# Storing the low part of one w1 tile 64 bytes lower, in both feed-forwards of a two-layer network

## The reference

```python
# layer 0
h = film(rmsnorm(x, norm1_w), cond, film1_w, film1_b)
x = x + attention(h)                      # one head of 256
h = film(rmsnorm(x, norm2_w), cond, film2_w, film2_b)
x = x + gelu(h @ mlp_w1 + mlp_b1) @ mlp_w2 + mlp_b2     # 256 -> 1024 -> 256
# layer 1
x = x + gate_msa * attention16(modulate(ln(x)))         # 16 heads of 16
x = x + gate_mlp * (gelu(modulate(ln(x)) @ w_mlp1 + b_mlp1) @ w_mlp2 + b_mlp2)
```

## The kernel before

|---|---|---|
| w1 hi | 221056 (128) | 106368 (128) |
| w1 lo | 212864 (128) | 114560 (128) |
| w2 hi | 202304 (64) | 140864 (64) |
| w2 lo | 194112 (64) | 149056 (64) |
| m_h_hi, m_h_lo (two each) | 97856, 99904, 101952, 104000 (all 64) | the same |
| g_hi, g_lo (four each) | all (128) | all (128) |

## Time and profile before

### The profile page before, as it was taken

The page is one execution under the profiler, slowest core; times in us unless marked ns, Lnnn a source line. Parts: engine busy times, 40 slices in busy tenths (PEclk is TensorE's granted clock), DMA queues, the critical chain, the costliest instruction groups (busy, mean ns, idle before and its releaser), DMA issues.

```text
span 1594.8 us, 42633 instructions
## 1 busy us (share of the span) xinstructions
PE 1560.0 (98%) x14314; PEld 1399.4 (88%) x14314; DVE 1307.9 (82%) x2953; ACT 846.7 (53%) x1696; POOL 483.1 (30%) x639
## 2 busy tenths in 40 slices
PE   8999999999999999999999999999997999999999
PEld 7999998999999998677777777777775999999999
DVE  5798888787777777788888888888885888888886
ACT  3566664343333343667777767776666333333333
POOL 2333322131111223243433434433333322222221
PEclk9999999999999999999999999999999999999999
DMA  5600002111111112333333333333331232222222
GB/s 175 216 21 20 20 20 72 66 43 52 40 53 39 53 41 65 107 107 98 108 106 106 112 96 106 105 102 111 100 104 63 80 100 92 94 90 94 89 94 68
DMA packets 147362, 132.72 MB, mean 83 GB/s; under 512 B 23552, under 2 KB 129984, under 8 KB 147280
## 3 DMA queue, kind: packets, MB, share of 16 engines
q1 hardware_dynamic: 147120, 131.61, 25.9%
q0 software_dynamic: 160, 0.04, 0.1%
HBM read 54.61 MB, written 24.54 MB: 50 GB/s over the span
## 4 chain that ended last, share of the span: by engine, by line
PE 89%; DVE 6%; issue 2%; DMA 1%; ACT 1%; SPq 0%; DVEq 0%; ACTq 0%; POOL 0%; POOLq 0%
PE bank L209 61%; PE bank L1733 8%; PE bank L1715 7%; PE bank L1677 5%; PE bank L1743 2%; PE bank L393 2%; DVE D_g_hi L1084 1%; PE bank L1751 1%; PE bank L765 1%; PE bank L465 1%; DVE D_g_lo L1086 1%; PE bank L191 1%; ACT D_g L1076 0%; PE bank L556 0%; DMA A_w_film<-in_L_cond_film_w 0%
## 5 line engine op out<-in xcount | busy, mean ns | idle before, releaser
L1824 ACT ACTIVATE C_probs<-bank 128x1024 f32<-128x1024 f32 x256 | 262.7, 1026 | 157.6 <-PE bank L1715 157.2
L1689 DVE TENSOR_REDUCE C_negmax<-bank 128x4 f32<-128x1024 f32 x248 | 303.4, 1223 | 48.5 <-PE bank L1677 44.6
L1076 ACT ACTIVATE D_g<-bank,D_bias 128x256 f32<-128x256 f32 x256 | 107.5, 472 | 223.0 <-PE bank L209 212.3
L1076 ACT ACTIVATE B_g<-bank,B_bias 128x256 f32<-128x256 f32 x256 | 107.5, 471 | 222.2 <-PE bank L209 222.2
L358 POOL TENSOR_TENSOR m_small<-m_small,consts 128x2 f32<-128x2 f32 x64 | 48.9, 763 | 476.9 <-DVE m_small L349 239.4
L209 PE MATMUL bank<-D_wt_w_hi,D_g_lo 128*128 128x256 f32 x512 | 144.7, 283 | 3.8 <-DVE D_g_lo L1086 3.4
L209 PE MATMUL bank<-B_wt_w_hi,B_g_lo 128*128 128x256 f32 x512 | 144.8, 283 | 3.2 <-DVE B_g_lo L1086 3.0
L1715 PEld LDWEIGHTS bank<-C_qs,C_kx 64*128 64x128 f32 x1024 | 77.3, 185 | 78.7 <-ACT C_probs L1824 46.0
L209 PE MATMUL bank<-m_h_hi,B_wt_w_lo 128*128 128x256 f32 x512 | 143.6, 281 | 0.0
L209 PE MATMUL bank<-B_wt_w_lo,B_g_hi 128*128 128x256 f32 x512 | 143.4, 280 | 0.0
L209 PE MATMUL bank<-B_wt_w_hi,B_g_hi 128*128 128x256 f32 x512 | 143.4, 280 | 0.0
(11 more groups left out here) (263 smaller groups left out, 4931.4 us busy)
## 6 DMA issues: line engine op xcount, KB each, us to landing
C_qs<-C_q_hi SPq DMA_DIRECT2D x128, 128.0 KB
C_kx<-C_k_hi SPq DMA_DIRECT2D x128, 128.0 KB, 2.6
C_qs<-C_q_lo SPq DMA_DIRECT2D x64, 128.0 KB
C_kx<-C_k_lo SPq DMA_DIRECT2D x64, 128.0 KB, 2.1
C_gbc<-mod_rows SPq DMA_DIRECT2D x32, 256.0 KB, 3.4
D_gbc<-mod_rows SPq DMA_DIRECT2D x32, 256.0 KB, 3.4
turned<-N_blocks SPq DMA_DIRECT2D x31, 256.0 KB, 2.0
N_back<-turned SPq DMA_DIRECT2D x124, 64.0 KB, 2.0
```

The lines of the kernel that those rows point to most:

```text
L1076: ins = eng.activation(o, p, func, bias=per_seq(bias1, 2 * u + d, b))
L1689: e_max.by(eng.tensor_reduce(m4[:, :, :, j], spair[:, :].rearrange("p (e q k) -> p e q k", e=2, q=TH), AX, ALU.max, negate=True))
L1824: e_exp.by(eng.activation(probs[t % NP][:, :], stpair[:, :], ACT.Exp, scale=scl))
```

## The change

In both feed-forwards the low part of w1 tile 0 is stored first in the buffer `lo`, and the other 15 tiles behind it with 16 elements (64 bytes) of unused room between. `lo` begins 64 bytes lower than before, so that tile 0 of it lies at remainder 64 and the other tiles lie, in B, exactly where they were. In D the buffers `lo` and `hi` change places: `lo` from 106304 (64; its other tiles from 106880, 128), `hi` from 114560 (128). To keep everything else in its place, the small buffer `consts` (32 bytes) is given up (its values move into unused columns of `a_small` and `m_small`), the gap of 64 bytes `gap2` goes, `gap_m` grows by 32 bytes, and the layer 1 `bcol` moves into the temporary room of phase B. w2, g, m_h and the buffers of C keep their addresses.

`emit_lo` makes two instructions instead of one for the part that holds tile 0 (128 columns, and 384 columns); the other parts stay one instruction each. Reading and order on PE are unchanged.

```diff
+LEAD, LEAD_GAP = (0,), 16
...
-            def __init__(self, sb, sem, name, view):
+            def __init__(self, sb, sem, name, view, lead=(), lo_first=False):
...
+                self.lead, self.rest = list(lead), [i for i in tiles if i not in lead]
+                self.rest_at = len(lead) * P + (LEAD_GAP if lead else 0)
...
+                n = self.t * self.N
+                if self.lo_first:
+                    self.lo = sb("wt_" + self.name + "_lo", [P, n + self.rest_at - len(self.lead) * P], F32R)
+                self.hi = sb("wt_" + self.name + "_hi", [P, n], F32R)
+                if not self.lo_first:
+                    self.lo = sb("wt_" + self.name + "_lo", [P, n + self.rest_at - len(self.lead) * P], F32R)
...
+                for start, group in ((0, self.lead), (self.rest_at, self.rest)):
+                    mine = [i for i in group if part * n <= i * P < (part + 1) * n]
...
+                    ins = eng.tensor_tensor(self.lo[:, o:o + len(mine) * P].rearrange("p (i c) -> p i c", c=P),
+                                            raw[:, src], hi[:, src].bitcast(F32), ALU.subtract)
+                ins.then_inc(self.s_lo, 1)
...
+                    o = self.lead.index(i) * P if i in self.lead else self.rest_at + self.rest.index(i) * P
+                return self.hi[:, c:c + n], self.lo[:, o:o + n]
...
-        scale1m, consts = sb("scale1m", [P, KT * NB]), sb("consts", [P, 8])
-        neghalf, one_rows, zero_col = consts[:, 0:TH], consts[:, TH:TH + 1], consts[:, TH + 1:TH + 2]
+        scale1m = sb("scale1m", [P, KT * NB])
+        neghalf, one_rows, zero_col = small["a_"][:, 22:24], small["m_"][:, 22:23], small["m_"][:, 23:24]
...
-                sb("gap_m", [P, 8])
+                sb("gap_m", [P, 16])
...
-                self.bcol = sb("bcol", [P, HT])
                 if not layer:
+                    self.bcol = sb("bcol", [P, HT])
                     sb("gap1", [P, 16])
-                self.w = [Weight(sb, sem, "w1", a[n1])]
+                self.w = [Weight(sb, sem, "w1", a[n1], LEAD, layer == 1)]
...
-                sb_tmp("next_rest", [P, 448])
+                sb_tmp("next_rest", [P, 448 - HT])
+                mlp.bcol = sb_tmp("next_bcol", [P, HT])
...
-            sb_near("gap2", [P, 16])
```

More of the change, by code:

```diff
@@ L147, in build @@
         class Weight:
-            def __init__(self, sb, sem, name, view):
+            def __init__(self, sb, sem, name, view, lead=(), lo_first=False):
                 self.view, self.t, self.N = view, view.shape[0] // P, view.shape[1]
+                tiles = range(self.t * self.N // P)
+                self.lead, self.rest = list(lead), [i for i in tiles if i not in lead]
+                self.rest_at = len(lead) * P + (LEAD_GAP if lead else 0)
+                self.lo_first = lo_first
                 self.name, self.raw = name, None
@@ L159, in place @@
             def place(self, sb):
-                self.hi = sb("wt_" + self.name + "_hi", [P, self.t * self.N], F32R)
-                self.lo = sb("wt_" + self.name + "_lo", [P, self.t * self.N], F32R)
+                n = self.t * self.N
[4 more added lines that the diff above has]
+                    self.lo = sb("wt_" + self.name + "_lo", [P, n + self.rest_at - len(self.lead) * P], F32R)
             def place_raw(self, sb):
@@ L182, in emit_lo @@
                     eng.wait_ge(self.s_read, readers)
-                eng.tensor_tensor(self.lo[:, c], self.raw[:, c], self.hi[:, c].bitcast(F32), ALU.subtract).then_inc(self.s_lo, 1)
-            def part(self, k, c0, n):
-                return self.hi[:, k * self.N + c0:k * self.N + c0 + n], self.lo[:, k * self.N + c0:k * self.N + c0 + n]
+                if not self.lead:
+                    eng.tensor_tensor(self.lo[:, c], self.raw[:, c], self.hi[:, c].bitcast(F32), ALU.subtract).then_inc(self.s_lo, 1)
+                    return
+                raw, hi = (t[:, :].rearrange("p (i c) -> p i c", c=P) for t in (self.raw, self.hi))
+                for start, group in ((0, self.lead), (self.rest_at, self.rest)):
+                    mine = [i for i in group if part * n <= i * P < (part + 1) * n]
+                    if not mine:
+                        continue
+                    step = mine[1] - mine[0] if len(mine) > 1 else 1
+                    src = slice(mine[0], mine[-1] + 1, step)
+                    o = start + group.index(mine[0]) * P
+                    ins = eng.tensor_tensor(self.lo[:, o:o + len(mine) * P].rearrange("p (i c) -> p i c", c=P),
+                                            raw[:, src], hi[:, src].bitcast(F32), ALU.subtract)
+                ins.then_inc(self.s_lo, 1)
+            def part(self, k, c0, n):
+                c = k * self.N + c0
+                o = c
+                if self.lead:
+                    assert n == P
+                    i = c // P
+                    o = self.lead.index(i) * P if i in self.lead else self.rest_at + self.rest.index(i) * P
+                return self.hi[:, c:c + n], self.lo[:, o:o + n]
         def shift_bias(eng, psum, col, w, c0, shift):
```

## The result

| | before | after |
|---|---|---|
| runs of the first measurement, us | 1600.56, 1588.55, 1587.48, 1587.78 | 1604.09, 1606.84, 1605.34, 1602.65 |
| median, us | 1588.16 | 1604.71 |
| span of the profiled execution, us | 1594.8 | 1602.3 |

The ratio is 1.0082, 95% interval 1.0048 to 1.0116: 0.8% longer, beyond the interval though inside the 1% that the prediction called about the same; 16.5 us between the medians, but only 7.5 us between the spans of the two profiled executions. The time lies outside the predicted range of 1586 to 1600 us.

A forecast was written before the change was run, and what follows sets the result against it. PE's stream of products was taken to bound the kernel. From the profiled 1596.58 us, B's long stretch -4.5, D's first sequences +1.7, D's end +0.6 and B's end +0.4 summed to -1.8: 1594.8 us, range 1586 to 1600.

The forecast's parts named there:

- The first product of a sequence: Both feed-forwards: new difference 0 turns the spacing over between 113 and 118 ns a product; two sequences take 22.21 us.
- the 55 places: Places in the earlier trace, outside the feed-forwards, where difference 0 turned the spacing over: 27 from 118, 28 from 113.
- The period of 256 bytes: Address differences were taken to repeat every 256 bytes, so the new 256 modulo 512 counted as a true 0.
- Cover in B: In B, DVE waits 2.5 us a sequence, so it can follow a PE gain of 0.43 us.
- B's long stretch: B, 338 to 587.5 us: 22 sequences go from 11.31 to 11.11 us each, -4.5 us.
- D's end: D, 1557.4 to 1594.8 us: three undisturbed sequences at 113 ns a product lose +0.6 us.
- B's start: B, 248 to 338 us: waits leave either spacing about half and half; 0, with 1.7 us to either side.
- D's loop: D, 1329 to 1557.4 us: waits for DVE draw the spacing anew; taken as 0, 1.1 us at most either side.
- The reading of the 8 us: Median 8.0 us below the profiled execution: the median runs were taken to have B at 113 ns a product.
- capture rival: Feed-forwards: difference 0 holds the stream at 118 ns a product and 113 is lost; +6.4, 1603.0 us; chance 0.13.
- addresses do nothing: Rival: the stream passes the new difference undisturbed and the time stays that of before, 1588.6 us; chance 0.12.
- the turning over: Main forecast: each difference 0 switches between 113 and 118 ns a product, so sequences alternate; 1594.8 us; chance 0.40.

The follow-up runs named there:

- f_own0: D's w1 tile 0 at 64 as in the change; from sequence 4 down 2's last product streams a w2 copy at remainder 0: 1598.34 us, one run.
- f_prev0: Moved buffers with tile 0 at remainder 128; in D from sequence 4 down 2's last product streams a w2 copy at 128: 1599.38 us beside 1596.92.
- s2: Low parts of w1 tiles 0, 2, 4, 6 at various remainders, without layer 0's second bias: 1589.87 us beside 1596.92, one run each.
- b_look2: The kernel before, unchanged, profiled again: 1593.46 us.
- b_look3: The kernel before, unchanged, profiled again: 1599.84 us.
- again_change: The change itself measured again on another chip, against the kernel before: 1604.12 us, ratio 1.0040.
- e_d_only: The change with tile 0 at remainder 64 in layer 1 only, 128 in layer 0: 1601.80 us, ratio 1.0017 to the kernel before.
- e_control: The change's moved buffers, but tile 0 at remainder 128, keeping address difference 64: 1599.97 us against 1600.04 before, ratio 0.9989.
- e_32: The change with tile 0 at remainder 96 in both layers, difference 32: 1590.76 us, ratio 0.9943 to the kernel before.
- best: Tile 0 at remainder 96 in D; in B in its own buffer at remainder 224, difference 160: 1590.19 us, ratio 0.9949.

## Why the prediction was wrong

- **The step that failed** is the one in "The first product of a sequence", where the own difference was called open and the new difference then taken for a true 0 like the 55 places. Those had the own difference 64, and were 0 modulo 512 against the product before. With both at 0 the stream doesn't turn over but is captured in 118: 100 of 100 and 108 of 108. The 55 places let the stream out of 118 at each of their 27 chances, the change at none of 108. Which of the two unlike properties does it, the own difference or the 256 modulo 512 against the product before, stays open: f_own0 (own 0, 64 before it) doesn't capture, f_prev0 (0 modulo 512 before it, own 64) doesn't either, both with the product of `twin` beside them, and 256 modulo 512 with an own difference of 64 was not run.
- **The period of 256 bytes** held for a stream that comes at 113: the 0 modulo 512 of s2 pushes it to 118 as the 256 of the change does. For a stream that comes at 118 it isn't tested.
- **Cover in B**: read rightly. In b_look2 B runs at 113 with PE busy for all of its 206.70 us, so DVE follows there.
- **B's long stretch**: -4.5 expected, 0 against the profiled execution (214.9 for 214.8 us), +8.2 against an execution at 113 (206.7 in b_look2, 19 sequences).
- **D, sequences 2 to 8**: +3.1 us for seven sequences, 0.44 each; I had +1.7 for eight by alternation. The size of a sequence was right, the alternation not.
- **D's end** (sequence 28 to the last product): 45.1 us before, 46.6 after; +1.5 for +0.6. This stretch is drawn too: b_look3, with difference 64, has 46.6.
- **D's first sequence** was to stay at 118 by its new difference of 192. In after, again_change and e_d_only it went from 118 to 113; the next first product took it back, so that nothing of it reaches the sum.
- **B's start**, taken as 0 with 1.7 to either side: 112.2 us before, 114.3 after. Over the ten profiles with difference 64 in layer 0 it is 111.6 to 113.8, mean 112.6; over the three with 0 114.1 to 114.4, so +1.7. Part of this is the clock and not the address. Five of the ten have a granted clock of 0.98 or 0.99 there and take 113.2 us in the mean, the other five have 1.00 and take 111.9; the three with 0 all have 0.99. At like clock the difference is 1.1 us. The waits still let the stream out at 113, but each first product now takes it back.
- **D's loop**: 0 expected, 217.1 to 217.4 us. Most of what PE loses in `up` 0 comes out of its waits for `D_g_lo`: PE is busy 1.2 us longer (215.97 for 214.80) and waits 1.5 us less. The lines of PE's waits for DVE over D's sequences 9 to 27 (total, times, longest), of after first, then of before:

```profile
PE bank L237 <- DVE D_g_lo L1114: 0.4, 1, 0.4
```

```profile
PE bank L209 <- DVE D_g_lo L1086: 1.9, 7, 0.4
```

- **The splitting of the low part**: the lines view has 6.2 us of POOL for D's w1 low instead of 5.9, and B's on DVE unchanged at 1.4. e_control has the moved buffers and one instruction, e_32 has the moved buffers and the two instructions of the change; neither shows a cost.
- **The reading of the 8 us** (1588 us are executions with B at 113) held: b_look2. I had not seen that D's first stretch is drawn as well; four of the five further profiles of the kernel before have it at 118.
- **The price of the capture rival** was 1603.0 us, measured 1604.7 and 1604.1. I gave it 0.13 because the earlier trace rows showed turns both ways, and had named the own difference as what they lacked. With that unlike row unresolved, the turning over was too sure at 0.40, and the range stopped at 1600 short of the one rival on the other side.
- **The rival "addresses do nothing"** fell: e_32 and the change differ in 32 bytes of one tile, with 1590.8 to 1591.1 us for one and 1604.1 for the other. The rule of two independent read ports in the Trainium skill ("TensorE: Matmul & The Clock Gate", section "Step-by-step: what each phase is for") doesn't cover this: the traces disagree by 4.5 ns a product (117.8 beside 113.3) between these two kernels.

The 16.5 us between the medians of the first measurement then follow from an execution with B and D at 113 as their "before": 8.2 (B, 19 sequences) + 3.1 (D) + 1.5 (D's end) + 1.7 (B's start, of which 0.6 is the clock) + 0.5 (B's end, 51.9 us before and 52.3 after) = 15.0 us. 1.5 us are left, within the scatter of C, which takes 612.9 to 616.7 us over the eighteen profiles (last product of B to first product of D's second sequence). That the three low runs had B at 113 isn't seen in their own traces; it is inferred from b_look2, and that D was at 113 in them as well only from the sum.

## What to carry to other kernels

When a stream of products can run at either of two spacings, time the kernel many times before judging a change of addresses, and read the spacing off the starts in each profile: the median of three runs of before was a draw, the kernel after was not. A row that differs from the case in a property (here two: the own difference, and 256 for 0 modulo 512) bounds nothing until that is tried; give the unlike case the weight of the like one. One tile of w1 was worth 13 us of 1600 here, by the 32 bytes between remainder 64 and 96.

## What the hardware showed that I had not expected

- One product in 96 can set the spacing of the other 95. At six differences from 32 to 224 bytes it costs 0 to 27 ns and holds 113; at 0 it holds 118, which is 0.43 us a sequence.
- The two draws of the kernel before (B's long stretch, D's first) stand from the last short wait of PE before them (in before at 348.2 us, left at 118; in b_look2 at 362.8 us, left at 113), and B drew the long one in 9 of the 10 profiles in which layer 0 has difference 64. Why it is drawn so often there, and in the first measurement seemingly in one run of four, stays open.
- Short stretches at half the clock fall in B's start in eleven of the eighteen profiles: beginning at 261 to 264 us, at 312 to 314 us, or (in best) at both. The other seven have none there. The window of again_change just after its first sequence of B:

```profile
262.30:266.00 3.70, 3.70 (x21) 3.70 (x20) 1.76 (x8) 0.84 (x2) 0.70 (x1) 0.54 0.27 95
```

  21 products in 3.7 us, at a granted clock of 0.54, near 1.2 instead of 2.4 GHz, where 118 each would need 2.5. The kernel after has one from 309 to 317 us (0.79 over the window), and PE was busy without a break, at a clock of 1.00, from 302.2 to 312.4 us just before the clock fell. In B's start one stretch costs about 1.3 us (113.2 for 111.9 us, above) and is part of the scatter that no address explains; I did not find what sets it off.
